# Output projection of a fused attention kernel: 64-deep products on two halves of the array instead of zero-padded 128-deep ones

## The reference, cut to what matters

```python
xn = (x - moving_mean) * rsqrt(moving_var + BN_EPS) * gamma + beta
q, k, v = xn @ Wq + bq, xn @ Wk + bk, xn @ Wv + bv
scores = einsum('bhid,bhjd->bhij', q, k) * 64 ** -0.5
out = einsum('bhij,bhjd->bhid', softmax(scores), v) @ Wo + bo
return xn + out
```

## Time and profile before

| What | us |
|---|---|
| runs shown | 5053.69, 5052.20, 5052.27 (median 5052.27) |
| the profiled execution's own time | 5052.57 |
| its span, first to last instruction | 5050.8 |
| PE busy | 5017.7 (99%) |
| POOL busy | 4860.0 (96%) |
| ACT busy | 4619.3 (91%) |
| DVE busy | 4168.3 (83%) |
| PEld busy | 4097.2 (81%) |

### The profile page before, as it was taken

The page is one execution under the profiler, slowest core; times in us unless marked ns, Lnnn a source line. Parts: engine busy times, 40 slices in busy tenths (PEclk is TensorE's granted clock), DMA queues, the critical chain, the costliest instruction groups (busy, mean ns, idle before and its releaser), DMA issues.

```text
span 5050.8 us, 171699 instructions
## 1 busy us (share of the span) xinstructions
PE 5017.7 (99%) x51224; PEld 4097.2 (81%) x51224; DVE 4168.3 (83%) x8226; ACT 4619.3 (91%) x19460; POOL 4860.0 (96%) x3080
## 2 busy tenths in 40 slices
PE   7999999999999999999999999999999999999999
PEld 6888888888888888888888888888888888888887
DVE  6888888888888888888888888888888888888887
ACT  7999999999999999999999999999999999999998
POOL 7999999999999999999999999999999999999998
PEclk9999999999999999999999999999999999999999
DMA  7888888888888888888888888888888888888886
GB/s 136 161 161 161 161 161 161 161 161 161 160 161 160 161 161 161 161 161 161 161 161 160 162 160 161 161 160 161 160 161 161 161 161 161 161 161 161 161 161 136
DMA packets 4294235, 806.26 MB, mean 160 GB/s; under 512 B 4294208, under 2 KB 4294208, under 8 KB 4294208
## 3 DMA queue, kind: packets, MB, share of 16 engines
q1 hardware_dynamic: 4294208, 805.93, 82.2%
HBM read 537.10 MB, written 268.44 MB: 159 GB/s over the span
## 4 chain that ended last, share of the span: by engine, by line
PE 99%; issue 0%; DVE 0%; SPq 0%; POOL 0%; ACT 0%; DMA 0%; POOLq 0%; DVEq 0%; ACTq 0%
PE score_ps L494 22%; PE u_ps L505 21%; PE probsT_ps L481 21%; PE g_ps L521 17%; PE o_ps L540 14%; PE o_ps L529 4%; POOL y L263 0%; DMA bias_col<-in_L_conv_bv 0%; ACT probs L294 0%; PE u_ps L470 0%; SPq L180 0%; SPq L178 0%; SPq L182 0%; ACT g L316 0%; POOL x_weighted L254 0%
## 5 line engine op out<-in xcount | busy, mean ns | idle before, releaser
L294 ACT ACTIVATE probs<-score_ps,neg_top 128x128 f32<-128x128 f32 x8192 | 2935.6, 393 | 2.5 <-DVE neg_top L426 2.5
L254 POOL TENSOR_TENSOR x_weighted<-x_in,row_weights 128x1024 f32<-128x1024 f32 x1024 | 2424.9, 2368 | 173.0 <-POOL x_scaled_rows L270 66.8
L294 ACT ACTIVATION_READ_ACCUMULATOR probs<-score_ps,neg_top 128x1 f32 x8192 | 1894.7, 231 | 0.0
L407 DVE TENSOR_REDUCE row_stat<-score_ps 128x8 f32<-128x1024 f32 x1024 | 1255.4, 1226 | 353.2 <-PE score_ps L494 353.2
L263 POOL TENSOR_TENSOR y<-attn,x_scaled_rows 128x512 f32<-128x512 f32 x1024 | 1307.6, 1277 | 13.6 <-DVE attn L401 13.6
L481 PE MATMUL probsT_ps<-ident,probs 128*128 128x128 f32 x8192 | 1286.5, 280 | 0.7 <-ACT probsT L308 0.7
L270 POOL TENSOR_TENSOR x_scaled_rows<-x_weighted,out_bias 128x512 f32<-128x512 f32 x1024 | 1224.2, 1196 | 0.4
L494 PE MATMUL score_ps<-xT,g 64*128 64x128 f32 x16384 | 1190.8, 285 | 2.0 <-ACT g L316 2.0
L505 PE MATMUL u_ps<-probsT,x_in 128*64 128x128 f32 x16384 | 1120.5, 279 | 0.0
L494 PEld LDWEIGHTS score_ps<-xT,g 64*128 64x128 f32 x16384 | 994.6, 187 | 128.4 <-ACT g L316 5.3
L401 DVE TENSOR_TENSOR attn<-o_ps,inv_sum 128x512 f32<-128x512 f32 x1024 | 707.9, 691 | 467.1 <-DVE inv_sum L446 391.9
(11 more groups left out here) (66 smaller groups left out, 1843.2 us busy)
## 6 DMA issues: line engine op xcount, KB each, us to landing
x_quads<-in_x SPq DMA_DIRECT2D x4096, 64.0 KB, 2.2
x_in<-in_x SPq DMA_DIRECT2D x1024, 256.0 KB, 2.9
out<-y SPq DMA_DIRECT2D x1024, 256.0 KB, 2.7
norm_row<-in_L_conv_gamma SPq DMA_DIRECT2D x1, 32.0 KB, 3.7
norm_row<-in_L_conv_beta SPq DMA_DIRECT2D x1, 32.0 KB, 3.7
norm_row<-in_L_conv_moving_mean SPq DMA_DIRECT2D x1, 32.0 KB, 4.2
norm_row<-in_L_conv_moving_var SPq DMA_DIRECT2D x1, 32.0 KB, 4.4
norm_row<-in_L_conv_bo SPq DMA_DIRECT2D x1, 32.0 KB, 4.7
```

The costliest lines, as they stand in the source:

```text
L254: nc.gpsimd.tensor_tensor(x_weighted[:, n % 2, :, 0:2 * C].rearrange("p s (h c) -> p s h c", h=2), x_in[:, n % 8, :, None, :].broadcast_to ...
L294: last = nc.scalar.activation(probs[:, n % 2, q, :], score_ps[n % 2][:, q // PAIRS, q % PAIRS * W:(q % PAIRS + 1) * W], ACT.Exp, bias=neg_ ...
L407: nc.vector.tensor_reduce(row_stat[:, s, :, ROW_MAX].rearrange("p (h k) -> p h k", h=2), score_ps[n % 2][:].rearrange("p h (k w) -> p h k ...
```

## The change

- `w_o` becomes [128, 64]: the same 64 by 64 block on both halves of the partitions, without zero blocks. One memset on POOL in the setup goes, and the two copies of L384 go into the one matrix.
- The output projection of a group, two 128-deep matmuls' worth of work per two pairs before, is now 8 matmuls of 64 deep, one for each pair k and half h: weights uT[half, k] (64 by 128), moving operand w_o[half] (64 columns). The half h = 0 writes into one bank, h = 1 into another, as the scores do. In passes: 16 of 64 moving columns in place of 8 of 128.
- All of it stands at the end of the step, behind the second transposes and ahead of the next step's scores. L529, the pair between g and the second transposes, is gone from there.
- `u_ps` and `o_ps` become the two banks of one tile `uo_ps`. The half h = 0 of o writes into the bank that also takes u. So u of group n now waits for `attn_kept` of group n-1 in place of `u_kept` of group n-1, and o waits for `u_kept` alone.
- DVE's attn reads the first 256 columns of the two banks, not the 512 of one.

```diff
-        w_o = sb("w_o", [128, 2, C])
+        w_o = sb("w_o", [128, C])
...
-        u_ps, g_ps, probsT_ps, o_ps = (psum(n) for n in ("u_ps", "g_ps", "probsT_ps", "o_ps"))
+        g_ps, probsT_ps = (psum(n) for n in ("g_ps", "probsT_ps"))
+        uo_ps = psum("uo_ps", (128, 2, 512))
+        u_ps, o_ps = uo_ps[:, 0, :], uo_ps[:, 1, :]
...
-            nc.gpsimd.memset(w_o[:], 0.0).then_inc(pool_const, 1)
...
-                chain(nc.vector.tensor_copy(w_o[p, h, :], u_ps[p, C:2 * C]))
+                chain(nc.vector.tensor_copy(w_o[p, :], u_ps[p, C:2 * C]))
...
-            o_rows = o_ps[:].rearrange("p (s c) -> p s c", s=GROUP)
+            o_rows = uo_ps[:, :, 0:PAIRS * C].rearrange("p h (k c) -> p h k c", k=PAIRS)
...
-                    nc.vector.tensor_tensor(attn[:, s], o_rows, inv_sum[:, s, :, None].broadcast_to([128, GROUP, C]),
+                    nc.vector.tensor_tensor(attn[:, s].rearrange("p (h k) c -> p h k c", h=2), o_rows,
+                                            inv_sum[:, s].rearrange("p (h k) -> p h k", h=2)[:, :, :, None].broadcast_to([128, 2, PAIRS, C]),
...
                     pe.wait_ge(probsT_b_kept[s], uses(r, n))
                     if exists(r, n - 1, peeled):
-                        pe.wait_ge(u_kept[parts(n - 1)], uses(r, n - 1))
+                        pe.wait_ge(attn_kept[parts(n - 1)], uses(r, n - 1))
...
-                n = t - 2
-                if exists(r, n, peeled):
-                    s = parts(n)
-                    pe.wait_ge(u_kept[s], uses(r, n))
-                    if exists(r, n - 1, peeled):
-                        pe.wait_ge(attn_kept[parts(n - 1)], uses(r, n - 1))
-                    nc.tensor.matmul(o_pairs[:, :, 0, :], uT[:, n % 2, 0, :], w_o_all, start=True, stop=True)
                 n = t - 1
...
                 n = t - 2
                 if exists(r, n, peeled):
                     s = parts(n)
-                    for k in range(1, PAIRS):
-                        last = nc.tensor.matmul(o_pairs[:, :, k, :], uT[:, n % 2, k, :], w_o_all,
-                                                start=True, stop=True)
+                    pe.wait_ge(u_kept[s], uses(r, n))
+                    for k in range(PAIRS):
+                        for h in range(2):
+                            half = slice(h * C, (h + 1) * C)
+                            last = nc.tensor.matmul(uo_ps[:, h, k * C:(k + 1) * C], uT[half, n % 2, k, :], w_o[half, :],
+                                                    start=True, stop=True)
                     last.then_inc(o_made[s], 1)
```

More of the change, by code:

```diff
@@ L125, in build @@
         PARAM_DMAS = 4 + 4 + 5 + 3
-        POOL_CONSTS = 3
+        POOL_CONSTS = 2
         class Turn:
@@ L474, in _ @@
             w_g_all = w_g[:].rearrange("p h c -> p (h c)")
-            w_o_all = w_o[:].rearrange("p h c -> p (h c)")
-            o_pairs = o_ps[:].rearrange("p (h k c) -> p h k c", h=2, k=PAIRS)
             def transposed_probs(n, first):
```

## The result

The changed kernel takes 5248.44 us (median of 4 runs, 5247.73 to 5249.07) against 5052.24 us before: 1.0388 times the time, 95% interval 1.0370 to 1.0406. That is 196 us more, 0.19 us in each of the 1024 steps. The forecast was slower, at 5186 us in a range of 5100 to 5240: the direction came out, the size did not, and the time lies 8 us above the range.

What follows compares the result with a forecast made beforehand. The prediction took PE to bound the kernel, at 4.89 us a step. Its terms, 0 + 0 + 0.11 + 0.02 = 0.13 us a step over 1024 steps, added 133 us to 5052.57: 5186 us, range 5100 to 5240.

Steps and rivals of the forecast that it cites:

- The floor under a shorter step: POOL's records cover 4.75 us a step, so a shorter PE step pays only down to that, some 0.14 us.
- the first rival: Pairs of o take half the time, POOL then decides: 4909 us, faster; chance 5%.
- Part 1: Output projection o on PE: loads of 128 weight columns set the pace, 8 pairs stay at 0.89 us, gain 0.
- The rival of pairs at half the time: In o, two array halves at once with half the moving columns each halve a pair's time: 4909 us; chance 5%.
- Part 2: The array-shape switch on PE moves from ahead of the scores to ahead of o: 0, with 0.02 us either way.
- Part 3: Second transposes on PE wait for ACT's copy with only g as cover: cost 0.11 us a step, lower bound 0.05.
- Part 4: PE's u waits for the previous group's attn, as its bank holds half of o: cost 0.02 us, bounds 0 and 0.07.
- No wait where I see one: Rival: g or the switch covers ACT's copy, or faster loads offset the handover; about 5053 us; chance 4%.
- the halves do not overlap: Rival on o: 16 passes at 0.11, 0.89 us more a step, 6100 us; chance 1%.
- The wait on attn is the larger one: Rival: attn takes longer or starts later, delaying u by 0.2 us in place of 0.02; 5370 us; chance 5%.
- What I said would show it: Chain through ACT's copy, second transposes 0.94 after g, u's load about 0.11 behind attn, a pair of o every 0.11.

Runs made afterwards that it cites:

- quads_os: The changed kernel with the matmuls of o and of the scores cut to 64 weight columns on four quarters of the array; 4857.69 us, ratio 0.9613.
- wide_b: The changed kernel with 128 moving columns in each of the 16 passes of o in place of 64; 5303.77 us, ratio 1.0495.
- swap_both: The changed kernel with two PE wait pairs reordered: attn_kept first ahead of u, probsT_a_kept first ahead of the second transposes; 5115.97 us, ratio 1.0124.
- order_b: The changed kernel with DVE's wait for y_found written before that for o_made, ahead of attn; 5276.65 us, ratio 1.0442.
- o_first: The changed kernel with o_made written as the first of DVE's three waits ahead of attn; 5189.48 us, ratio 1.0270.
- quads_swap: quads_os with the reordered waits of swap_both and o_first added; 4860.92 us, ratio 0.9619.
- quads_all: quads_os with attn cut into two instructions and y_found waited for ahead of o_made; 4854.81 us, ratio 0.9607.
- quads_o: The changed kernel with only the matmuls of o cut to 64 weight columns on four quarters of the array; 4914.97 us, ratio 0.9727.

## Why the prediction was wrong, point by point

**What bounds the kernel.** Right: PE was the bound and stayed it, and a longer PE step was paid in full, 0.19 x 1024 = 195 us. The floor under a shorter step, POOL's 4.75, was 0.05 too high: POOL's instructions can start every 4.70 (quads_os). The time given for the first rival, 4909, was too high by as much.

**Part 1, the passes of o.** Right, gain 0. Shown from two sides: twice the moving columns cost nothing on the array (1.98 for o and scores together), and half the weight columns per load, on quarters, took 0.4 us out of o (1.04 to 0.62). The row that carried the argument was the setup's. The rival of pairs at half the time has fallen for halves of the array with 128 weight columns. The up to 2x of the Trainium skill ("TensorEngine Tiling (Array Packing)", section "Theoretical Speedup") showed in this kernel only where the weight columns of a load were halved too, which is what the quarters do: 0.56 us of loads for 1.00.

**Part 2, the switch.** Right, 0: o plus scores are 1.99 us for 1.98. The price divided otherwise than I wrote, o 1.04 and scores 0.95 in place of 1.09 and 0.89; wide_b, with 128 moving columns, shows exactly 1.09 and 0.89. With 64 columns the first pair behind the switch is shorter (0.16 for 0.21), and the scores' first pair gives it back (0.17 for 0.11).

**Part 3, the hole where L529 stood.** Right, 0.11 us: the kernel with this edit alone is 114 us slower, and swap_both, with the handover at 0.05, takes 65 us back, which is the lower bound that part 3 named.

**Part 4, u behind attn.** This is the step that failed. It said 0.02 us with bounds of 0 and 0.07; the measured term is 78 / 1024 = 0.076. The mechanism was right, three pieces of its size were not:

- The last pass of o starts at P = 2502.30 + 1.11 - 0.27 = 2503.14 and attn at 2503.51, P + 0.37, as before the change. I had moved attn to P + 0.32 for the shorter pass, but the distance does not depend on the moving columns: it is P + 0.38 with 128 of them too (wide_b). The scores' last pair was later against P by the same 0.05 (P + 0.94), so that of the two shifts nearly nothing remained.
- Part 3 counted 0.03 from the load to the matmul behind a wait; part 4 forgot it. The load came at 2504.32, 0.03 later than the switch alone would allow (scores' last pair at 2504.08, plus 0.21 is 2504.29), and the matmul at 2504.35. Together 0.06 in every step.
- The first step of each turn of the loop is 0.10 us longer, and attn starts 0.10 late there. Averaged over eight steps that is 0.0125, 13 us in all. I had read one ordinary step and taken each of its intervals for fixed. In the kernel before the delay was there as well, but it held nothing on the chain, so no interval of the chain could have shown it. DVE's timeline could: attn starts 0.37 behind the last pass of o in seven steps of eight and 0.47 in the eighth (pass at 2534.12, attn at 2534.59).

**The range.** The sum's own upper bound was 5257 us and held the result; the range was cut to 5240 inside it. With part 4 at its upper bound of 0.07 the sum is 0.18, 5237 us, and the last 11 us are about what the turns of the loop cost (13).

**The rivals.** "No wait where I see one" and "the halves do not overlap" have fallen. "The wait on attn is the larger one" was nearest: with 0.076 in place of 0.02 it gives 5052.57 + 1024 x (0.11 + 0.076) = 5243. Of its two reasons one fell, as attn kept its 0.69, and one held: attn starts later than P + 0.32, and later again once in a turn. Its size of 0.2 was far off.

**What I said would show it.** The distance of 0.94 from g to the second transposes is there, and u's load 0.12 behind attn; a pair of o starts every 0.11. The chain through ACT's copy is not: it names PE alone, because g's record hides the hole.

## What to carry to other kernels

Halving the depth of a matmul saves nothing while its weight load sets the pace; count columns of weights against moving columns before cutting either, and cut the one that is longer (here quarters in place of halves, for o and the scores: 4858 us against 5052). Before moving an instruction, ask what round trip through another engine it fills, and do not expect the chain to show the hole. Where two waits stand ahead of an instruction on a tight path, write the one that comes last first, and read the first step of a loop turn as well as an ordinary one. A floor that another engine sets is read from the distance of its starts where it does not wait, not from the length of its records.

## What the runs showed of the hardware that was not expected

- The order in which two waits are written changed the handover from ACT or DVE to PE's weight load from 0.11 to 0.05 us (measured behind ACT in swap_both): 132 us in this kernel from two swapped pairs of lines (5248.44 to 5115.97).
- attn started 0.10 us late once in eight steps, with a register instruction on DVE's sequencer ahead of it: 13 us, once u waited for attn. Where the instruction ran before o_made (order_b) the long step was gone, and where it still ran behind it (o_first) the 0.09 stayed.
- POOL's records of x_weighted averaged 2368 ns in the kernel before, 3090 in quads_os, 3317 in quads_swap and 2381 in quads_all, while the next instruction started 2.3 us behind it in all of them. What lengthens the records is open; a step of 4.70 us was reached with the long records and with the short.
- Four quarters of the array load and multiply at once: 32 loads of 64 by 64 in 0.56 us, and 32 passes of o on the chain in 0.62 (quads_o).
